# Max and exp of a softmax straight from PSUM, and a new order of work in a slot

## The chip, the cores and the metric

The kernel runs on one core of one Trainium2 chip. The metric is the device time of one execution in microseconds (us).

The engines are written as in the profile: PE is TensorE (matmuls; its weight loads are the row PEld), DVE is VectorE, ACT is ScalarE, POOL is GpSimd, SP is SyncE. Each works through its own list of instructions in the order in which the kernel wrote them, and they meet only at semaphores. The kernel gives matmuls eight banks of PSUM.

## The reference, cut to what matters

64 sequences of 128 tokens with 160 channels, each with a context of 77 rows of 256 channels, go through two layers. All is fp32.

```
# first layer ("l0"): 20 heads of 64, twice (self-attention, then attention to the context), then GEGLU
sim  = q @ k.T * 64**-0.5              # self: 128 columns a head; context: 77
attn = softmax(sim);  x = x + (attn @ v) @ wo + bo
x    = (h * gelu(gate)) @ w2 + b2 + x

# second layer ("l1"): 20 heads of 8; 73 text rows and 4 image rows of the context
p_t  = softmax(q @ k_t.T * 8**-0.5)    # 73 columns a head
qsem = l2norm(p_t @ text);  sem = qsem @ l2norm(image).T
p_ip = softmax(q @ k_ip.T * 8**-0.5 + 0.5 * sem) * mask
out  = (p_t @ v_t + p_ip @ v_ip) @ W_out + b_out + x
```

## The kernel before

**Groups, slots and units.** The 64 sequences are worked through in 16 groups of four. A *unit* is the softmax of four heads: a unit of the first layer is two heads of two sequences (40 a group: 20 of the self-attention, 20 of the context), a unit of the second layer is four heads of one sequence (20 a group). Time is cut into *slots*, `STEP = 60` a group, one unit in each. `UNIT_AT` says which: the second-layer units of a group stand in slots 4, 5, 7, 8, 10, 11, 13, 14, 16, 17, 22, 24, 27, 30, 33, 37, 42, 47, 50 and 53 of the group *after* it, and first-layer units in the other 40. For the last group the 20 second-layer units stand alone (slots 4 to 13 and 20 to 29), with no first-layer work around them.

**The pipeline of a unit.** Every engine runs one loop over the slots `t`, and in each slot it does a different stage of several units. Before, for the unit of slot u: PE computes its scores into one of two banks `PS` in slot u-1; DVE takes the maximum, subtracts it into the buffer `SE` (four buffers) and, for a second-layer unit, copies the image scores away (`softmax_in`, slot u); ACT takes the exponential of `SE` in place (`exp`, slot u); for first-layer units DVE sums and inverts (`prob_sums`) and POOL multiplies (`normalise`), slot u+1; PE transposes the probabilities into the bank `PT` (`probs_transposed`, slot u+2), ACT copies them to `PTs` (`pt_out`); PE multiplies them by the values into the bank `PV` (`probs_v`, slot u+3); for a first-layer unit ACT copies `PV` out (`ot_out`, slot u+4) and PE applies `wo`; for a second-layer unit DVE reads `PV` (`unit_out`, slot u+4: a reciprocal, three small products, one product over 292 columns that ends in `on_done`, one sum of squares).

**Product bank.** `PVS` has one bank. So `probs_v` of a unit waits until the unit before it has been read: by ACT (`ots_done`) or, where that was a second-layer unit, by DVE (`on_done`, the fifth instruction of `unit_out`, L940).

**Jobs.** Everything else that PE computes goes through three general banks `PG` in the order of `JOBS`: the projections of q and k for the first-layer unit two slots ahead (`qk`), and the "late" jobs at a slot's end: values (`v`, one for two units), transposes of the normalised input (`xT`), feed-forward (`ff`, `down`, in slots 55 to 58 and 68 to 71 of a group), and the second layer's own. In slots 55 to 57 and 68 to 70 ACT goes between Gelu and Exp, each with a table load.

**Order before, within slot t.** PE: scores(t+1), transposes(t-2), qk(t+2), wo(t-4), products(t-3), late jobs. ACT: ot_out(t-4), pt_out(t-2), qk copies(t+2), exp(t), tails, late jobs. DVE: unit_out(t-4), softmax_in(t), prob_sums(t-1), block_out(t-4), late jobs, layer norms, tails. POOL: normalise(t-1), layer norms, and once per sequence of the second layer one `pow` over 20 columns.

## Time and profile before

| | |
|---|---|
| median of 3 runs | 4817.66 us (4814.41 to 4827.26) |
| the profiled execution: time, span | 4820.58 us, 4818.8 us |
| busy share of the span: PE, DVE, ACT, POOL | 89%, 63%, 51%, 21% |
| mean granted clock of PE | 0.925 of full speed |
| first scores of the groups 8 and 9 | 2326.6 us and 2620.1 us |

The profiled execution lasted 1.8 us more than its span, and is 3 us above the median. A group takes 293.5 us in the middle of the run (287 us for some). A busy PE is not PE at its peak, since matmuls overlap. The granted clock is 1.0 (2.4 GHz) or 0.5 (1.2 GHz); a value between them is a mixture over the stretch.

### The profile page before, as it was taken

Reading aid. Unit: us, or ns where it says so; the run is one execution under the profiler, and the core shown is the slowest. Engines: PE = TensorE matmul, PEld = TensorE weight load, DVE = VectorE, ACT = ScalarE, POOL = GpSimd, SP = SyncE. Lnnn points to the kernel's source line nnn. Section 1 sums busy time; section 2 is a strip of 40 time slices with the busy share of each in tenths; the row PEclk is TensorE's granted clock in tenths of the full one; section 3 lists DMA queues with packets and bytes.
Section 4 is the critical chain, followed back from the end, with each engine's and each line's share of the span. In section 5 each row is a group of like instructions: output and inputs, shape, how many; then the busy total and the mean of one; then the engine's idle time right before and its main releaser. Section 6 shows DMA issues by size and latency. Waiting matters only on the chain.

```text
span 4818.8 us, 85960 instructions
## 1 busy us (share of the span) xinstructions
PE 4271.6 (89%) x31232; PEld 3694.5 (77%) x31232; DVE 3024.9 (63%) x9036; ACT 2435.6 (51%) x5493; POOL 1013.4 (21%) x1079
## 2 busy tenths in 40 slices
PE   1898988999899998999999899898999999999997
PEld 1787877878787787877878788787877878777776
DVE  3556675666666666665666656666676666656654
ACT  2455554545555554554545545455554545545442
POOL 0222222122222222222122212221122122212211
PEclk9999999999999999989999999999999999899995
DMA  4000000000000000000000000000000000000000
GB/s 113 3 3 7 3 7 3 6 4 3 7 3 6 4 4 6 3 6 3 6 4 3 6 3 6 4 3 6 4 5 4 4 5 3 7 2 5 4 3 3
DMA packets 34030, 34.27 MB, mean 7 GB/s; under 512 B 4336, under 2 KB 31824, under 8 KB 33616
## 3 DMA queue, kind: packets, MB, share of 16 engines
q1 hardware_dynamic: 26752, 25.47, 1.9%
q10 hardware_dynamic: 6864, 3.30, 0.4%
q8 instruction: 257, 4.21, 0.4%
q14 instruction: 157, 1.29, 0.1%
HBM read 23.52 MB, written 5.24 MB: 6 GB/s over the span
## 4 chain that ended last, share of the span: by engine, by line
PE 67%; DVE 18%; issue 7%; ACT 3%; POOL 3%; POOLq 0%; DVEq 0%; DMA 0%; ACTq 0%
PE PT L595 8%; PE PW L558 6%; PE PS L571 6%; PE PG L451 5%; PE PV L609 5%; PE PV L619 5%; PE PG L443 5%; PE PS L580 4%; DVE mx L896 3%; PE PG L426 3%; PE PG L429 3%; PE PG L427 3%; PE PG L428 3%; DVE SE L900 2%; POOL SE L1037 2%
## 5 line engine op out<-in xcount | busy, mean ns | idle before, releaser
L1037 POOL TENSOR_TENSOR SE<-SE,rs 128x512 f32<-128x512 f32 (+1 forms) x640 | 559.0, 873 | 3168.1 <-DVE rs L918 3168.0
L699 ACT ACTIVATE PTs<-PT 77x512 f32<-77x512 f32 (+2 forms) x960 | 571.3, 595 | 1073.8 <-PE PT L595 1073.2
L706 ACT ACTIVATE SE<-SE 128x308 f32<-128x308 f32 (+2 forms) x960 | 491.4, 512 | 488.8 <-DVE SE L900 367.8
L595 PE MATMUL PT<-ident,SE 128*128 128x128 f32 (+2 forms) x3840 | 653.7, 297 | 79.1 <-POOL SE L1037 79.0
L595 PEld LDWEIGHTS PT<-ident,SE 128*128 128x128 f32 (+2 forms) x3840 | 482.7, 153 | 294.9 <-POOL SE L1037 151.7
L827 DVE COPY v_sb<-PG 128x512 f32<-128x512 f32 (+1 forms) x320 | 220.1, 688 | 746.5 <-PE PG L451 416.2
L571 PE MATMUL PS<-qk 128*128 128x154 f32 (+1 forms) x2560 | 583.7, 350 | 59.5 <-ACT qk L660 30.4
L609 PE MATMUL PV<-PTs,v_sb 128*64 128x128 f32 (+1 forms) x5120 | 441.4, 295 | 120.6 <-issue 87.3
L900 DVE TENSOR_TENSOR SE<-PS,mx 128x308 f32<-128x308 f32 (+2 forms) x960 | 522.2, 544 | 33.0
L896 DVE TENSOR_REDUCE mx<-PS 128x4 f32<-128x308 f32 (+2 forms) x960 | 508.8, 530 | 18.1 <-PE PS L571 15.1
L558 PE MATMUL PW<-w_o,OTs 128*128 128x160 f32 x2560 | 500.4, 321 | 10.2 <-ACT OTs L691 10.2
L571 PEld LDWEIGHTS PS<-qk 128*128 128x128 f32 x2560 | 404.7, 192 | 122.1 <-issue 40.7
L609 PEld LDWEIGHTS PV<-PTs,v_sb 128*64 128x64 f32 (+1 forms) x5120 | 284.3, 142 | 231.5 <-issue 181.6
L660 ACT ACTIVATE qk<-PG 64x164 f32<-64x164 f32 (+1 forms) x1280 | 426.9, 334 | 7.5
L658 ACT ACTIVATE qk<-PG 128x256 f32<-128x256 f32 x640 | 246.0, 384 | 351.2 <-PE PG L443 194.1
L558 PEld LDWEIGHTS PW<-w_o,OTs 128*128 128x128 f32 x2560 | 403.7, 206 | 16.1 <-ACT OTs L691 15.2
L619 PE MATMUL PV<-gv,PTs 73*128 73x86 f32 x2560 | 363.3, 289 | 54.1 <-DVE SE L940 48.3
L619 PEld LDWEIGHTS PV<-gv,PTs 73*128 73x128 f32 x2560 | 350.3, 209 | 66.8 <-ACT PTs L699 50.1
L580 PE MATMUL PS<-kbd,q1T 32*128 32x308 f32 x640 | 282.4, 524 | 105.0 <-DVE SE L900 79.2
L913 DVE TENSOR_REDUCE sums<-SE 128x4 f32<-128x512 f32 (+1 forms) x640 | 364.6, 570 | 12.0 <-ACT SE L706 12.0
L443 PE MATMUL PG<-cT,w_kc 128*128 128x164 f32 x1920 | 270.8, 280 | 0.0
L451 PE MATMUL PG<-w_vc,cT 128*77 128x256 f32 x1920 | 261.3, 285 | 0.0
(204 smaller groups left out, 8133.8 us busy)
## 6 DMA issues: line engine op xcount, KB each, us to landing
xres<-in_x_dram SPq DMA_DIRECT2D x32, 160.0 KB, 2.4
out_dram<-x SPq DMA_DIRECT2D x64, 80.0 KB, 1.6
shared<-in_ctx_dram SPq DMA_DIRECT2D x32, 154.0 KB
w_o<-in_L_xattn_a_wo_dram ACTq DMA_DIRECT2D x2, 800.0 KB, 11.5
SE<-in_L_xattn_a_wq_dram SPq DMA_DIRECT2D x2, 640.0 KB, 4.7
qk<-in_L_xattn_a_wq_dram SPq DMA_DIRECT2D x8, 160.0 KB, 4.7
SE<-in_L_xattn_a_wk_dram SPq DMA_DIRECT2D x2, 640.0 KB, 4.0
SE<-in_L_xattn_a_wv_dram SPq DMA_DIRECT2D x2, 640.0 KB, 3.8
```

Of the source, the lines that this page charges most:

```text
L443: last = mm(ps, w[:, c, hw, c0:c0 + 128], cT[:, c, hc, HB * TS * h:HB * TS * (h + 1)], start=(c == 0 and i == 0), stop=(c == 1 and i == 2))
L451: last = mm(ps, cT[:, c, hc, TS * b:TS * b + rows], w[:, c, hw, c0:c0 + n], start=(c == 0 and i == 0), stop=(c == 1 and i == 2))
L558: last = mm(PW[:, C * b:C * b + C], OTs[:, n % 2, 128 * b:128 * b + 128], w_o[n // U0][:, p, :], start=(p == 0 and b == 0), stop=(p == NP ...
L571: last = mm(ps[:, 2 * J * b:2 * J * b + 2 * J], qk[:, n % 2, 0, 128 * b:128 * b + 128], qk[:, n % 2, 1:3, kstep * b:kstep * b + J], start= ...
L595: last = tr(PT[0:J, 128 * i:128 * i + 128], SE[:, place % 4, J * i:J * i + J], ident[:, :])
L609: last = mm(PV[DH * e:DH * e + DH, 128 * b:128 * b + 128], v_sb[0:J, n // 2 % 2, b, 2 * (n % 2) + e, :], PTs[0:J, place % 2, 128 * i:128 * ...
L619: last = mm(PV[:, GV * i + off:GV * i + off + GS + D1], PTs[0:TT, place % 2, 128 * i:128 * i + 128], gv[:, b % 2, 2 * w + i // 2, off:off ...
L699: a_(PTs[0:J, place % 2, :], PT[0:J, :], ACT.Copy).then_inc(S["pts_done"], 1)
L706: a_(e, e, ACT.Exp, scale=scale).then_inc(S["exp_done"], 1)
L896: v.tensor_reduce(mx[:, place % 2, :], sc[:, :, 0:J], AX, ALU.max).then_inc(S["mx_done"], 1)
L900: last = v.tensor_tensor(e.rearrange("p (i j) -> p i j", j=J), sc[:, :, 0:J], mx[:, place % 2, :].unsqueeze(2).to_broadcast([128, 4, J]), ...
L1037: gp.tensor_tensor(e, e, rs[:, n % 2, :].unsqueeze(2).to_broadcast([128, 4, J]), ALU.mult)\
```

## The change

No count of banks changes: three `PG` and one `PV` stand in both kernels. What changes:

- **Softmax.** DVE writes the maximum negated and no longer subtracts. ACT computes exp(score + bias) straight from the bank `PS` with four instructions, one a head, whose bias is a column of `mx`. The scale moves into the copies of q (`SCALE0`, `SCALE1`). `sub_done` is gone: the bank `PS` is released by `exp_done`, and for second-layer units also by `sip_in`, the copy of the image scores.
- **Lags.** Transposes come one slot after a unit's slot instead of two, products two instead of three, outputs three instead of four (`PT_LAG`, `PV_LAG`, `OUT_LAG`); sums and normalisation move from slot t+1 to slot t, the maximum from t to t-1, `v` jobs from t+1 to t, and the tails of a sequence follow its last unit one slot sooner.
- **Order.** PE: scores(t+1), qk(t+2), transposes(t-1), wo(t-3), products(t-2), late. ACT: ot_out(t-3), exp(t), qk copies(t+2), pt_out(t-1), tails, late. DVE: prob_sums(t), softmax_in(t+1), unit_out(t-3), block_out(t-3), the rest as before. POOL: normalise(t), layer norms, and norms_of(t-3).
- **Norms.** The `pow` over 20 columns per sequence becomes one over 4 columns after each second-layer unit (`norms_of`, into the new buffer `n20`).

```diff
+    PT_LAG, PV_LAG, OUT_LAG = 1, 2, 3
...
-            return STEP * (g + 1) + l1_slots(g)[W1 * b + W1 - 1] + 6
+            return STEP * (g + 1) + l1_slots(g)[W1 * b + W1 - 1] + OUT_LAG + 2
...
-            [(t + 1, ("v", u[1], u[2] // 2)) for t, u in UNIT_AT.items() if u[0] == "l0" and u[2] % 2 == 0]
+            [(t, ("v", u[1], u[2] // 2)) for t, u in UNIT_AT.items() if u[0] == "l0" and u[2] % 2 == 0]
...
                 def scores(u):
                     place, (layer, g, n) = PLACE[u], u
                     if place >= 2:
-                        pe.wait_ge(S["sub_done"], place - 1)
+                        pe.wait_ge(S["exp_done"], place - 1)
+                        layer0, g0, n0 = UNITS[place - 2]
+                        if layer0 == "l1":
+                            pe.wait_ge(S["sip_in"], l1_count(g0, n0))
...
                     if t + 1 in UNIT_AT:
                         scores(UNIT_AT[t + 1])
-                    if t - 2 in UNIT_AT:
-                        probs_transposed(UNIT_AT[t - 2])
                     for name in qk_at(t):
                         job(name)
-                    if l0_at(t - 4) is not None:
-                        wo(*l0_at(t - 4)[1:])
-                    if t - 3 in UNIT_AT:
-                        probs_v(UNIT_AT[t - 3])
+                    if t - PT_LAG in UNIT_AT:
+                        probs_transposed(UNIT_AT[t - PT_LAG])
+                    if l0_at(t - OUT_LAG) is not None:
+                        wo(*l0_at(t - OUT_LAG)[1:])
+                    if t - PV_LAG in UNIT_AT:
+                        probs_v(UNIT_AT[t - PV_LAG])
...
-                        a_(qk[:, i % 2, 0, :], ps[:, 0:HT], ACT.Copy)
+                        a_(qk[:, i % 2, 0, :], ps[:, 0:HT], ACT.Copy, scale=SCALE0)
...
                 def exp(u):
                     place, (layer, g, n) = PLACE[u], u
-                    act.wait_ge(S["sub_done"], place + 1)
-                    J, scale = (K0[n // U0], SCALE0) if layer == "l0" else (TT, SCALE1)
-                    e = SE[:, place % 4, 0:4 * J]
-                    a_(e, e, ACT.Exp, scale=scale).then_inc(S["exp_done"], 1)
+                    act.wait_ge(S["mx_done"], place + 1)
+                    if place >= 4:
+                        act.wait_ge(S["pt_done"], place - 3)
+                        layer0, g0, n0 = UNITS[place - 4]
+                        if layer0 == "l1":
+                            act.wait_ge(S["qq_done"], l1_count(g0, n0))
+                    J, step = (K0[n // U0],) * 2 if layer == "l0" else (TT, T)
+                    if layer == "l1":
+                        act.wait_ge(S["sip_in"], l1_count(g, n))
+                    for i in range(4):
+                        last = a_(SE[:, place % 4, J * i:J * i + J], PS[place % 2][:, step * i:step * i + J], ACT.Exp,
+                                  bias=mx[:, place % 2, i:i + 1])
+                    last.then_inc(S["exp_done"], 1)
...
-                    if l0_at(t - 4) is not None:
-                        ot_out(UNIT_AT[t - 4])
-                    if t - 2 in UNIT_AT:
-                        pt_out(UNIT_AT[t - 2])
+                    if l0_at(t - OUT_LAG) is not None:
+                        ot_out(UNIT_AT[t - OUT_LAG])
+                    if t in UNIT_AT:
+                        exp(UNIT_AT[t])
                     for name in qk_at(t):
                         job(name)
-                    if t in UNIT_AT:
-                        exp(UNIT_AT[t])
+                    if t - PT_LAG in UNIT_AT:
+                        pt_out(UNIT_AT[t - PT_LAG])
...
-                    v.tensor_reduce(mx[:, place % 2, :], sc[:, :, 0:J], AX, ALU.max).then_inc(S["mx_done"], 1)
-                    dve.wait_ge(S["mx_done"], place + 1)
-                    if place >= 4:
-                        dve.wait_ge(S["pt_done"], place - 3)
-                    last = v.tensor_tensor(e.rearrange("p (i j) -> p i j", j=J), sc[:, :, 0:J],
-                                           mx[:, place % 2, :].unsqueeze(2).to_broadcast([128, 4, J]), ALU.subtract)
+                    v.tensor_reduce(mx[:, place % 2, :], sc[:, :, 0:J], AX, ALU.max, negate=True).then_inc(S["mx_done"], 1)
...
-                    if t - 4 in UNIT_AT and l0_at(t - 4) is None:
-                        unit_out(UNIT_AT[t - 4])
-                    if t in UNIT_AT:
-                        softmax_in(UNIT_AT[t])
-                    if l0_at(t - 1) is not None:
-                        prob_sums(UNIT_AT[t - 1])
+                    if l0_at(t) is not None:
+                        prob_sums(UNIT_AT[t])
+                    if t + 1 in UNIT_AT:
+                        softmax_in(UNIT_AT[t + 1])
+                    if t - OUT_LAG in UNIT_AT and l0_at(t - OUT_LAG) is None:
+                        unit_out(UNIT_AT[t - OUT_LAG])
...
+                def norms_of(g, k):
+                    b, w = k // W1, k % W1
+                    pool.wait_ge(S["qq_done"], l1_count(g, k))
+                    if w == 0 and GB * g + b >= 2:
+                        pool.wait_ge(S["tail_part"], 4 * (GB * g + b - 2) + 1)
+                    gp.tensor_tensor(n20[:, b % 2, 4 * w:4 * w + 4], qq[:, b % 2, 4 * w:4 * w + 4], p_half[:, 0:4], ALU.pow)\
+                        .then_inc(S["n20_done"], 1)
...
-                    if l0_at(t - 1) is not None:
-                        normalise(UNIT_AT[t - 1])
+                    if l0_at(t) is not None:
+                        normalise(UNIT_AT[t])
...
-                    for g, b, part in tails_at(t):
-                        if part == -1:
-                            pool.wait_ge(S["qq_done"], W1 * (GB * g + b + 1))
-                            gp.tensor_tensor(r20[:, 0, :], qq[:, b % 2, :], p_half[:, :], ALU.pow).then_inc(S["n20_done"], 1)
+                    if t - OUT_LAG in UNIT_AT and l0_at(t - OUT_LAG) is None:
+                        norms_of(*UNIT_AT[t - OUT_LAG][1:])
```

## Rows read from the trace of the kernel before

**Rows 1.** The page, part 1: busy us (share of the span) and instructions.
```profile
PE 4271.6 (89%) x31232; PEld 3694.5 (77%) x31232; DVE 3024.9 (63%) x9036; ACT 2435.6 (51%) x5493; POOL 1013.4 (21%) x1079
```

**Rows 2.** The view of the cores: span, and mean granted TensorE clock.
```profile
core 0: 4818.8 us, clock 0.925
```

**Rows 3.** The waits of PE: total us, times, longest us.
```profile
PE PV L609 <- issue: 87.3, 60, 2.2
PE PS L580 <- DVE SE L900: 79.2, 105, 1.8
PE PT L595 <- POOL SE L1037: 79.0, 123, 2.7
PE PV L619 <- DVE SE L940: 48.3, 48, 2.7
...
PE PS L571 <- ACT qk L660: 30.4, 52, 1.2
...
PE PS L571 <- DVE SE L900: 17.9, 19, 1.0
```

**Rows 4.** Groups of DVE by form: busy us, mean ns of one, idle before.
```profile
L900 DVE TENSOR_TENSOR SE<-PS,mx 128x512 f32<-128x512 f32 x320 | 221.3, 692 | 11.1
L896 DVE TENSOR_REDUCE mx<-PS 128x4 f32<-128x512 f32 x320 | 216.7, 677 | 15.8 <-PE PS L571 14.8
...
L896 DVE TENSOR_REDUCE mx<-PS 128x4 f32<-128x308 f32 x320 | 148.8, 465 | 1.4 <-PE PS L571 0.3
...
L918 DVE RECIPROCAL rs<-sums 128x4 f32<-128x4 f32 x640 | 114.0, 178 | 22.0
```

**Rows 5.** Groups of ACT by form, same columns.
```profile
L706 ACT ACTIVATE SE<-SE 128x512 f32<-128x512 f32 x320 | 201.7, 630 | 282.8 <-DVE SE L900 279.3
...
L706 ACT ACTIVATE SE<-SE 128x308 f32<-128x308 f32 x320 | 146.9, 459 | 93.0 <-DVE SE L900 88.5
...
L706 ACT ACT_TABLE_LOAD x96 | 123.2, 1283 | 1.7
...
L668 ACT ACTIVATE shared<-PG,b 128x256 f32<-128x256 f32 x160 | 72.8, 474 | 38.4 <-PE PG L429 37.1
```

**Rows 6.** Groups of POOL by form, same columns.
```profile
L1057 POOL TENSOR_TENSOR r<-qq,p_half 128x20 f32<-128x20 f32 x64 | 226.6, 3540 | 97.1 <-DVE qq L942 97.1
...
L1019 POOL TENSOR_TENSOR rstd<-vp,p_mhalf 128x2 f32<-128x2 f32 x96 | 68.7, 716 | 8.0
```

**Rows 7.** Timeline of PE, slots 40 and 42 of group 8: start us, us, what.
```profile
2528.07 0.69 PE L571 MATMUL PS<-qk 128*128 128x154 f32 x4
...
2528.59 0.60 PE L595 MATMUL PT<-ident,SE 128*77 128x128 f32 x4
...
2529.03 0.71 PE L558 MATMUL PW<-w_o,OTs 128*128 128x160 f32 x4
...
2536.93 0.37 PE L426 MATMUL PG<-nT,w_q_hi 128*128 128x256 f32 x1
...
2538.14 0.74 PE L558 MATMUL PW<-w_o,OTs 128*128 128x160 f32 x4
```

**Rows 8.** Timeline of PE, a slot that begins with first-attention scores.
```profile
2393.77 1.03 PE L571 MATMUL PS<-qk 128*128 128x256 f32 x4
2394.63 0.60 PE L595 MATMUL PT<-ident,SE 128*128 128x128 f32 x4
```

**Rows 9.** Timeline, a wait for the product bank.
```profile
2469.41 0.18 DVE L928 RECIPROCAL rr<-PV 128x4 f32<-128x4 f32 x1
...
2469.88 0.45 DVE L940 TENSOR_TENSOR SE<-PV,SE 128x292 f32<-128x292 f32 x1
...
2470.43 0.66 PE L609 MATMUL PV<-PTs,v_sb 128*64 128x128 f32 x8 [2.24 <-issue]
```

**Rows 10.** Windows after that wait, and around one of 1.78 us: busy, PEclk, DMA.
```profile
2475.00:2480.00 5.00, 5.00 (x35) 4.34 (x34) 0.30 (x3) 2.52 (x6) 1.04 (x1) 0.62 0.00 0
2590.00:2595.00 5.00, 3.22 (x31) 2.92 (x31) 3.68 (x13) 2.20 (x6) 0.24 (x1) 1.00 0.00 0
```

More of the change, by code:

```diff
@@ L131, in xattn_program @@
         r20 = sb("r20", [128, 4, H])
+        n20 = sb("n20", [128, 2, H])
         o1 = sb("o1", [128, 2, H, D1])
@@ L268, in xattn_program @@
                  "qk_done", "v_done",
-                 "s_done", "mx_done", "sub_done", "exp_done", "sum_done", "p_done", "pt_done", "pts_done", "pv_done", "rs_done", "rr_done",
+                 "s_done", "mx_done", "sip_in", "exp_done", "sum_done", "p_done", "pt_done", "pts_done", "pv_done", "rs_done", "rr_done",
                  "on_done", "ots_done", "wo_done", "x_done",
@@ L670, in job @@
                     elif kind == "q1":
-                        a_(q1T[:, i, :, :].rearrange("p r n -> p (r n)"), take(name)[:, :], ACT.Copy)\
+                        a_(q1T[:, i, :, :].rearrange("p r n -> p (r n)"), take(name)[:, :], ACT.Copy, scale=SCALE1)\
                             .then_inc(S["q1_done"], 1)
@@ L905, in softmax_in @@
                             dve.wait_ge(S["job_full"], JOB[("ipT",) + divmod(GB * g + b - 2, GB)] + 1)
-                        last = v.tensor_copy(sip[:, b % 2, 4 * w:4 * w + 4, :], sc[:, :, TT:T])
-                    last.then_inc(S["sub_done"], 1)
+                        v.tensor_copy(sip[:, b % 2, 4 * w:4 * w + 4, :], sc[:, :, TT:T]).then_inc(S["sip_in"], 1)
                 def prob_sums(u):
@@ L947, in image_scores @@
                     if part == 0:
-                        dve.wait_ge(S["n20_done"], j + 1)
-                        then(v.tensor_tensor(r20[:, 1, :], r20[:, 0, :], rr[:, k, :], ALU.mult))
+                        dve.wait_ge(S["n20_done"], W1 * (j + 1))
+                        then(v.tensor_tensor(r20[:, 1, :], n20[:, k, :], rr[:, k, :], ALU.mult))
                         then(v.tensor_scalar(r20[:, 2, :], r20[:, 1, :], EPS_L2, None, ALU.max))
@@ L955, in image_scores @@
                                                     r20[:, 3, :].unsqueeze(2).to_broadcast([128, H, NIP]), ALU.mult, ALU.mult))
-                        v.scalar_tensor_tensor(e, e, SCALE1, sem4[:, k, :, :], ALU.mult, ALU.add)\
+                        v.tensor_tensor(e, e, sem4[:, k, :, :], ALU.add)\
                             .then_inc(S["tail_part"], 1)
@@ L978, in _ @@
                 for t in range(FIRST, LAST):
-                    if t - 4 in UNIT_AT and l0_at(t - 4) is None:
-                        unit_out(UNIT_AT[t - 4])
-                    if t in UNIT_AT:
-                        softmax_in(UNIT_AT[t])
-                    if l0_at(t - 1) is not None:
-                        prob_sums(UNIT_AT[t - 1])
-                    if l0_at(t - 4) is not None and l0_at(t - 4)[2] % NP == NP - 1:
-                        block_out(*l0_at(t - 4)[1:])
+                    if l0_at(t) is not None:
[4 more added lines that the diff above has]
+                        unit_out(UNIT_AT[t - OUT_LAG])
+                    if l0_at(t - OUT_LAG) is not None and l0_at(t - OUT_LAG)[2] % NP == NP - 1:
+                        block_out(*l0_at(t - OUT_LAG)[1:])
                     for g, h in preps_at(t):
```

1 line of the change is left out of this document (removed).

## Prediction

> **What bounds the kernel now.** I read the page's busy times first, then the view of the cores, the waits of PE, the timeline of two groups, and the windows around its stalls. The reader is to see in turn: who is the bound, how fast it is clocked, whom it waits for, what stands ahead of that in the other engine's queue, and what a stall does to the clock.
>
> PE is busy 4271.6 of 4818.8 us and no other engine comes near [rows 1]. So the end is set by PE's list of work, PE's stalls, and PE's clock. The mean granted clock is 0.925 [rows 2]; with levels 1.0 and 0.5 that is (1 - 0.925) / 0.5 = 15% of the span at the lower one, some 720 us, and about half of it, 360 us, is what the clock costs. The change alters no matmul. It can win or lose only in the stalls and, through them, the clock.
>
> The stalls fall into two families [rows 3]:
> - *Softmax not ready.* Scores wait for the subtraction that frees their bank: 79.2 + 17.9 = 97.1 us. Transposes wait for POOL's product: 79.0 us. Scores wait for the copies of q and k: 30.4 us. Together 206.5 us.
> - *Product bank not free.* The second-layer products wait 48.3 us for DVE's L940, the read that ends in `on_done`. The 87.3 us called "issue" ahead of L609 are the same wait as I read them: in the timeline L940 ends at 2470.33 and the products start at 2470.43, after 2.24 us [rows 9]. Together 135.6 us, or 8.5 us a group.
>
> **The work added and removed.** DVE loses the subtraction: 960 instructions, of 692 ns in the 512-wide form [rows 4] and less in the others; with about 0.55 us for the mean that is some 520 us, and DVE falls from 63% to about 52%. It isn't the bound, so this is worth nothing by itself; what counts is where DVE is late.
>
> ACT replaces one exponential of 630 or 459 ns [rows 5] by four. The trace has none of these, so I bound them. From the two widths the cost is (630 - 459) / (512 - 308) = 0.84 ns a column; the Gelu, which like the new exponential reads PSUM and takes a bias per partition, costs 474 ns at 256 columns, hence about 366 ns at 128 and 324 ns at 77. Four end to end are at most 1.46 and 1.30 us; at least they cost what the one instruction costs now, 0.63 and 0.46. Back-to-back instructions overlap a little, so I take 1.3 and 1.15 us, near the upper end. Added: 960 times 0.65 to 0.7 us, some 640 us; ACT rises from 51% to about 64%. It lies beside PE's work, unless ACT's order makes the copies of q and k late (a rival below). Table loads (1283 ns) stay as many, since only the first of the four needs one.
>
> POOL: `pow` takes 716 ns over 2 columns and 3540 over 20 [rows 6], so about 1.03 us over 4; 320 of these instead of 64 long ones are 330 us against 227. POOL is at 21%, and the long one, which stood in the way of the next normalisation, is gone. The lags, the `v` job a slot sooner and the folded scales cost nothing in work: the same instructions are issued, and no DMA moves apart from the stores, one slot sooner after each sequence.
>
> **What goes away.** Scores(t+1) now wait for exp(t-1), which comes a whole slot before. The transposes get the sums of their own slot and stand behind qk, so they come about 1.2 us later in PE's slot. I take away 90% of 97.1 + 79.0, and half of the 30.4: 158 + 15 = -173 us.
>
> **What grows: the wait for the one product bank.** In slot t PE's products(t-2) need `on_done` of the unit of slot t-3 when that is a second-layer unit: 20 times a group. Before, the matching `unit_out` was DVE's *first* item in the slot. Now it stands behind prob_sums(t), which waits for exp(t), and behind the maximum of the unit t+1, whose scores PE only begins in this slot. PE's own position in the slot is unchanged. Worked out from the slot's start T:
>
> - Slot 40 (first-layer context unit; unit 37 is second-layer; no qk, no wo). PE: scores 0.52 us, transposes 0.44 [rows 7], so it wants the product bank at T + 0.96. DVE: ACT finishes the preceding `pt_out` at about T + 0.15, exp(40) at T + 1.3; sums 0.47 (width as the maximum's 465 ns) and reciprocal 0.18 make about 2.0; maximum 0.47 [rows 4] makes 2.5; `unit_out` up to `on_done` takes 2470.33 - 2469.41 = 0.92, with semaphores 1.05 [rows 9], so 3.5. PE waits 2.5 us.
> - Slots where t is itself a second-layer unit have no sums. With self-attention scores next (0.86 us [rows 8], results some 0.2 later), maximum 0.68 and `unit_out` 1.05 give T + 2.9. Without a qk job PE is there at 1.3 and waits 1.6 us (slots 8, 11, 14: 4.8 us). With one (1.21 us, [rows 7], self-attention's about 1.0) it waits 0.4 to 0.6 or not at all (slots 7, 10, 13, 16, 17, 27, 30, 33, 50, 53: 3.8 us).
> - The seven slots of the first kind by the same sum: 19: 1.8; 20: 2.1; 25: 2.7; 36: 1.0; 40: 2.5; 45: 2.4; 56: 3.0 (here exp stands behind Gelus and a table load of 1.28 [rows 5]). Sum 15.5 us. What differs among them: 19, 20 and 25 are 512 wide (exp 1.3, sums and reciprocal 0.86, maximum 0.68); in 19, 36 and 56 a qk job keeps PE busy for 1.0 to 1.2 us of it; in 20 and 36 exp is done before T, and DVE is held by the copy of the values instead, until about T + 0.9.
>
> Total 24 us a group at full clock; at the lower clock, 15% of the time, PE arrives later, so I take 22. Against 8.5 now: +13.5 x 16 = +216 us.
>
> **The clock.** After the 2.24 us stall above the window 2475 to 2480 shows a granted clock of 0.62; around the stall of 1.78 us it stays 1.00 [rows 10]. So a longer stall is dearer than its own length. The new sum has nine stalls of 1.6 us and more a group. Now 720 / 16 = 45 us a group are spent at the lower clock; I put 6 to 7 us more: half of it, times 16, is +50 us.
>
> The Trainium skill, "TensorE: Matmul & The Clock Gate", section "HAM oscillation — how this bites in real kernels", says that regular idle gaps return the clock to half rate again and again. By it each of the nine stalls would bring one drop, which is the third rival below.
>
> **The end.** The last group's 20 second-layer units stand alone; the wait grows there too, by about 1 us in some 15 slots, against the last `pow` (2.5 us less) and a slot less of lag: +10 us.
>
> **Sum.** 4820.6 (the profiled execution's time, 3 us above the median) - 173 + 216 + 50 + 10 = 4923 us, and 4920 against the median: slower by 2.1%. Its own range is 4835 to 5000.
>
> **Rivals.**
> - *Faster: `unit_out` isn't late enough to matter.* DVE has 0.55 us a slot less to do and ACT may be done with exp(t) well before T. If the wait grows by 4 us a group instead of 13.5, that is +64; with -173 and a fifth of the clock's 360 us given back (-72), and nothing at the end, 4640 us. It decides from a growth below 11 us a group (173 / 16), and more surely below 8. For it: the backlog of DVE causes the present stalls, and each slot of backlog now holds one subtraction less. Against: the sum for slot 40 holds even with DVE idle before it. Range 4560 to 4805. Chance 0.31.
> - *Same: both families cancel.* PE's list stays at 4271.6 us and the stalls only move. 4818, chance 0.10. The Trainium skill, "Perfetto Trace Analysis", section "Identifying Performance Opportunities", holds that improvement comes from the most-contended engine; by that rule, with PE's work untouched, moving work from DVE to ACT gives this time.
> - *Much slower: the clock.* If each of the nine long stalls brings 7 us at the lower level (63 a group instead of 45, of which half, 9 us, is time and 3 of it are in the forecast) and the stalls are a third larger (+7 a group), that is 4923 + 16 x (6 + 7) = 5130 us. Chance 0.10.
> - *Much slower: ACT.* qk copies now stand behind exp(t). If they end 0.3 us after PE wants to begin the next scores in most of the 640 first-layer slots, +190 us on the forecast: 5110. Against it: exp(t) should end at T + 1.7 with ot_out ahead, before the qk job is through at about T + 2. Chance 0.06.
>
> **How the numbers follow.** The forecast has 0.43. About 0.3% is what a measurement of this kernel can tell from no change. Slower: 0.43 + 0.10 + 0.06 = 0.59; same 0.10; faster 0.31. The range 4640 to 5060 leaves out some 0.1 at either end.
>
> **What would show it.** Right: "issue" or L940 ahead of PE's product matmuls (L609, L619 of before) at some 300 to 380 us in PE's waits instead of 135.6; a wait of over 2 us in slots 25, 40 and 45 of each group; DVE's order there sums, maximum, reciprocal; waits of scores and of transposes below 50 us in all; the four exponentials together 1.1 to 1.3 us; ACT at 64%. Wrong: if DVE's `on_done` in slot 40 comes less than 2 us after the slot's scores begin, the forecast's main term falls; if the mean clock rises above 0.94, the clock's sign is wrong; if ACT's copies of q and k head the waits, it is the last rival.

## The result and the profile after

The changed kernel takes 4655.07 us (median of 4 runs, 4645.55 to 4656.96) against 4816.03 us: ratio 0.9662, 95% interval 0.9635 to 0.9689. It is 3.4% faster. I had forecast 2.1% slower; the time lies at the lower end of the range.

The profiled execution took 4653.59 us. The page's part 1 (it answers to [rows 1]) and the view of the cores ([rows 2]):

```profile
PE 4146.7 (89%) x31232; PEld 3600.3 (77%) x31232; DVE 2535.2 (54%) x8076; ACT 2832.9 (61%) x8373; POOL 1106.4 (24%) x1335
```

```profile
core 0: 4651.9 us, clock 0.949
```

The span fell by 4818.8 - 4651.9 = 166.9 us. It splits in two, because both kernels run the same 31232 matmuls. PE's idle time (span less busy) went from 547.2 to 505.2 us: -42. PE's busy time went from 4271.6 to 4146.7 us: -125, and that is the clock. A stretch at half clock costs half its length, so the clock costs (1 - mean) x span: 0.075 x 4818.8 = 361 us before, 0.051 x 4651.9 = 237 us after, -124.

PE's waits, in the columns of [rows 3]. L615 and L625 are the products of first- and second-layer units, L601 the transposes, L577 the first layer's scores:

```profile
PE PV L615 <- ACT PTs L705: 155.4, 103, 2.7
...
PE PV L615 <- issue: 91.5, 106, 3.0
PE PV L625 <- DVE SE L948: 85.7, 73, 3.1
PE PV L625 <- issue: 13.1, 17, 1.2
...
PE PT L601 <- POOL SE L1053: 7.8, 10, 1.3
PE PS L577 <- ACT qk L666: 5.2, 9, 1.1
```

The softmax family of the prediction has all but gone: 206.5 us became 7.8 + 5.2 = 13. The rows ahead of products sum to 345.7 us (347 with a row of 1.5). Three releasers are named, but in the trace every one of these 301 gaps ends 0.1 to 0.2 us after L948, the `on_done` of the changed kernel: all of them are the wait for the product bank. Slot 40 of group 8, the slot that the prediction worked out, in the timeline (start us, us, engine, line, what):

```profile
2443.36 0.95 ACT L719 ACTIVATE SE<-PS,mx 128x77 f32<-128x77 f32 x4
...
2443.60 0.72 PE L577 MATMUL PS<-qk 128*128 128x154 f32 x4
...
2444.16 0.60 PE L601 MATMUL PT<-ident,SE 128*77 128x128 f32 x4
2444.34 0.47 DVE L921 TENSOR_REDUCE sums<-SE 128x4 f32<-128x308 f32 x1 [1.02 <-ACT SE L719]
...
2444.85 0.18 DVE L926 RECIPROCAL rs<-sums 128x4 f32<-128x4 f32 x1
2444.95 0.45 DVE L910 TENSOR_REDUCE mx<-PS 128x4 f32<-128x308 f32 x1
...
2445.31 0.17 DVE L936 RECIPROCAL rr<-PV 128x4 f32<-128x4 f32 x1
...
2445.77 0.45 DVE L948 TENSOR_TENSOR SE<-PV,SE 128x292 f32<-128x292 f32 x1
...
2446.32 0.66 PE L615 MATMUL PV<-PTs,v_sb 77*64 77x128 f32 x8 [1.56 <-ACT PTs L705]
```

T is 2443.60, where PE starts the scores of the slot. The four exponentials end at T + 0.71, the sums run at T + 0.74, the reciprocal, the maximum at T + 1.35, `unit_out` from T + 1.71, L948 ends at T + 2.62, and PE's products start at T + 2.72 after 1.56 us. The order is the one forecast and PE's own arrival too (2446.32 - 1.56 = T + 1.16, by 0.96); ACT was 0.6 us sooner than I had put it, so the stall is 1.6 us and not 2.5.

The new instructions, ACT and POOL by form (columns of [rows 5]). I had put four exponentials at 1.3 us (128 columns) and 1.15 us (77); from the first's start to the fourth's end they took 1.14 and 0.97 us (medians of 320; 0.95 in slot 40). So ACT's busy time rose by 397 us (2435.6 to 2832.9) where I had put 640. The `pow` had been put at 1.03 us:

```profile
L719 ACT ACTIVATE SE<-PS,mx 128x128 f32<-128x128 f32 x1280 | 363.6, 373 | 22.3 <-DVE qq L950 14.6 <-DVE mx L910 7.5
L719 ACT ACTIVATE SE<-PS,mx 128x77 f32<-128x77 f32 x1280 | 309.7, 332 | 11.1 <-DVE mx L910 10.4
```

```profile
L1045 POOL TENSOR_TENSOR n<-qq,p_half 128x4 f32<-128x4 f32 x320 | 323.4, 1011 | 836.2 <-DVE qq L950 836.2
```

And the clock, in windows (us, busy of PE, PEld, DVE, ACT, POOL, then the granted clock, DMA). Before, around a wait of 1.43 us ahead of second-layer scores, whose timeline row comes first:

```profile
2345.49 1.14 PE L580 MATMUL PS<-kbd,q1T 32*128 32x308 f32 x2 [1.43 <-issue]
```

```profile
2340.00:2345.00 5.00, 4.06 (x33) 3.36 (x31) 4.29 (x10) 2.35 (x6) 0.29 (x2) 1.00 0.00 0
2345.00:2350.00 5.00, 4.51 (x19) 3.08 (x20) 4.24 (x13) 1.99 (x5) 1.91 (x2) 0.57 0.00 0
2350.00:2355.00 5.00, 5.00 (x19) 3.95 (x20) 3.09 (x11) 0.82 (x2) 1.87 (x4) 0.50 0.02 5
```

After, around one of its long waits:

```profile
2386.57 0.66 PE L615 MATMUL PV<-PTs,v_sb 128*64 128x128 f32 x8 [2.62 <-issue]
```

```profile
2385.00:2390.00 5.00, 3.43 (x28) 2.87 (x28) 3.56 (x14) 2.28 (x8) 2.35 (x3) 1.00 0.00 0
2390.00:2395.00 5.00, 4.58 (x41) 4.27 (x39) 2.98 (x12) 2.81 (x10) 0.73 (x1) 1.00 0.00 0
```

A wait of 1.43 us in the kernel before is followed by some 10 us at or near half clock, through a window in which PE is busy for all its 5 us. One of 2.62 us in the changed kernel leaves the clock at 1.00. So a single stall's length doesn't fix its price. But the second case is an exception, as all stretches at half clock show when they are counted in the two traces, from the first scores to those of the last group (103.5 to 4371.2 us before, 103.2 to 4213.9 after). Each is set against the last wait of PE, of over 0.15 us, that began before it; every stretch begins during that wait or at most 2.1 us after its end.

| | before | after |
|---|---|---|
| stretches at half clock | 83, 546 us in all | 67, 314 us in all |
| mean length of a stretch | 6.6 us | 4.7 us |
| its last wait is ahead of scores or transposes | 77 | 0 |
| its last wait is ahead of products | 6 | 67 |
| two or more waits in the 5 us before it | 59 | 0 |
| waits over 2 us that are such a last wait | 6 of 16 | 38 of 42 |
| waits of 1.6 to 2 us, the same | 2 of 31 | 23 of 33 |
| waits of 1 to 1.6 us | 37 of 75 | 6 of 67 |
| waits of 0.5 to 1 us | 38 of 224 | 0 of 67 |

In the changed kernel long waits, each alone, bring the falls of the clock. In the kernel before most falls come behind short waits that stand close together, and the last of them is nearly always one for the softmax; in 30 of the 83 the longest of the waits in the 5 us before is one ahead of products. The last group, where the mean clock is 0.81 in both, adds much the same to each (175 and 166 us at half clock). So the clock's gain lies in the middle of the run.

### The profile page after: what moved, and what is told of

It reads as the page before. It is cut to its first block, busy times and chain, and to the rows that moved or that the text cites. A ratio compares the mean times of both kernels' runs of the same rounds, so it can differ in the third digit from the quotient of the medians.

```text
span 4651.9 us, 88382 instructions
## 1 busy us (share of the span) xinstructions
PE 4146.7 (89%) x31232; PEld 3600.3 (77%) x31232; DVE 2535.2 (54%) x8076; ACT 2832.9 (61%) x8373; POOL 1106.4 (24%) x1335
## 3 DMA queue, kind: packets, MB, share of 16 engines
q14 instruction: 174, 1.43, 0.1%
## 4 chain that ended last, share of the span: by engine, by line
PE 77%; DVE 8%; issue 6%; ACT 6%; POOL 2%; ACTq 0%; DMA 0%; DVEq 0%; POOLq 0%
PE PS L577 10%; PE PV L615 8%; PE PT L601 8%; PE PW L561 7%; PE PG L454 6%; PE PV L625 6%; PE PG L446 5%; PE PG L429 4%; PE PS L586 4%; PE PG L432 3%; PE PG L430 3%; PE PG L431 3%; ACT SE L719 2%; PE PG L509 2%; PE PG L478 2%
## 5 line engine op out<-in xcount | busy, mean ns | idle before, releaser
L719 ACT ACTIVATE SE<-PS,mx 128x128 f32<-128x128 f32 (+2 forms) x3840 | 978.1, 343 | 81.5 <-DVE sip L915 45.3
L615 PE MATMUL PV<-PTs,v_sb 128*64 128x128 f32 (+1 forms) x5120 | 429.7, 288 | 246.9 <-ACT PTs L705 155.4
L601 PE MATMUL PT<-ident,SE 128*128 128x128 f32 (+2 forms) x3840 | 616.6, 286 | 7.9 <-POOL SE L1053 7.8
L577 PE MATMUL PS<-qk 128*128 128x154 f32 (+1 forms) x2560 | 603.9, 359 | 5.6 <-ACT qk L666 5.2
L615 PEld LDWEIGHTS PV<-PTs,v_sb 128*64 128x64 f32 (+1 forms) x5120 | 278.0, 138 | 368.6 <-issue 184.8
L601 PEld LDWEIGHTS PT<-ident,SE 128*128 128x128 f32 (+2 forms) x3840 | 471.6, 151 | 72.8 <-issue 43.7
L1045 POOL TENSOR_TENSOR n<-qq,p_half 128x4 f32<-128x4 f32 x320 | 323.4, 1011 | 836.2 <-DVE qq L950 836.2
L842 DVE COPY v_sb<-PG 128x512 f32<-128x512 f32 (+1 forms) x320 | 219.9, 687 | 493.9 <-PE PG L454 308.2
L561 PE MATMUL PW<-w_o,OTs 128*128 128x160 f32 x2560 | 472.9, 309 | 9.7 <-ACT OTs L697 9.6
L577 PEld LDWEIGHTS PS<-qk 128*128 128x128 f32 x2560 | 415.0, 196 | 65.6 <-issue 43.8
L625 PE MATMUL PV<-gv,PTs 73*128 73x86 f32 x2560 | 355.6, 285 | 100.3 <-DVE SE L948 85.7
L625 PEld LDWEIGHTS PV<-gv,PTs 73*128 73x128 f32 x2560 | 339.1, 203 | 121.1 <-issue 85.6
L561 PEld LDWEIGHTS PW<-w_o,OTs 128*128 128x128 f32 x2560 | 383.7, 198 | 16.3 <-ACT OTs L697 16.1
L697 ACT ACTIVATE OTs<-PV 128x256 f32<-128x256 f32 x640 | 242.4, 379 | 134.7 <-PE PV L615 127.3
L454 PE MATMUL PG<-w_vc,cT 128*77 128x256 f32 x1920 | 280.6, 298 | 0.0
L586 PE MATMUL PS<-kbd,q1T 32*128 32x308 f32 x640 | 266.8, 498 | 11.7 <-issue 11.7
## 6 DMA issues: line engine op xcount, KB each, us to landing
w_o<-in_L_xattn_a_wo_dram ACTq DMA_DIRECT2D x2, 800.0 KB, 11.7
```

The source lines that it names most:

```text
L454: last = mm(ps, cT[:, c, hc, TS * b:TS * b + rows], w[:, c, hw, c0:c0 + n], start=(c == 0 and i == 0), stop=(c == 1 and i == 2))
L561: last = mm(PW[:, C * b:C * b + C], OTs[:, n % 2, 128 * b:128 * b + 128], w_o[n // U0][:, p, :], start=(p == 0 and b == 0), stop=(p == NP ...
L577: last = mm(ps[:, 2 * J * b:2 * J * b + 2 * J], qk[:, n % 2, 0, 128 * b:128 * b + 128], qk[:, n % 2, 1:3, kstep * b:kstep * b + J], start= ...
L586: last = mm(ps[:, 0:4 * T], q1T[row:row + 32, h, r, 128 * (b % HB):128 * (b % HB) + 128], kbd[row:row + 32, r, b % HB, :, :].rearrange("p ...
L601: last = tr(PT[0:J, 128 * i:128 * i + 128], SE[:, place % 4, J * i:J * i + J], ident[:, :])
L615: last = mm(PV[DH * e:DH * e + DH, 128 * b:128 * b + 128], v_sb[0:J, n // 2 % 2, b, 2 * (n % 2) + e, :], PTs[0:J, place % 2, 128 * i:128 * ...
```

## The experiments

Times are medians; each ratio is to the kernel before, run on the same chip. Line numbers differ a little from one version to the next.

**out_first: `unit_out` back in front.** All else as changed.

```diff
+                    if t - OUT_LAG in UNIT_AT and l0_at(t - OUT_LAG) is None:
+                        unit_out(UNIT_AT[t - OUT_LAG])
                     if l0_at(t) is not None:
                         prob_sums(UNIT_AT[t])
                     if t + 1 in UNIT_AT:
                         softmax_in(UNIT_AT[t + 1])
-                    if t - OUT_LAG in UNIT_AT and l0_at(t - OUT_LAG) is None:
-                        unit_out(UNIT_AT[t - OUT_LAG])
```

> The changed kernel with unit_out moved back to the first place of DVE's slot; all else as changed. Theory 1 (the product bank is held too long because unit_out stands third): nearly all stalls of PE in the changed kernel stand ahead of products (347 us of PE's waits); with unit_out first they fall to 100 to 170 us, while waits for scores and transposes rise from 13 to at most 60 us. PE's idle time falls by 130 to 200 us, and if each us less of stall gives back half a us by the clock, the kernel takes 4350 to 4480 us. Rival (the order is neutral: what unit_out gains, the sums and the normalisation lose, and transposes wait instead): 4640 to 4670 us, with over 150 us of waits ahead of transposes.

Measured: 4325.02 us, ratio 0.8971 (0.8952 to 0.8990). The page's part 1 and the waits:

```profile
PE 4024.6 (93%) x31232; PEld 3493.4 (81%) x31232; DVE 2540.2 (59%) x8076; ACT 2822.8 (65%) x8373; POOL 1100.0 (25%) x1335
```

```profile
PE PV L625 <- DVE SE L948: 46.2, 40, 2.7
PE PV L615 <- ACT PTs L705: 38.7, 31, 1.6
PE PV L615 <- issue: 34.8, 68, 1.1
PE PT L601 <- POOL SE L1053: 12.7, 25, 1.3
...
PE PV L625 <- issue: 6.1, 16, 0.7
```

Waits ahead of products fell from 347 to 125.8 us, and transposes rose only from 7.8 to 12.7. PE's idle time fell by 505.2 - 291.8 = 213 us, the clock (0.978) gave 237 - 95 = 142 us. The waits are in the expected range; the idle time fell by more than the 130 to 200 us expected and the time is below the 4350 to 4480, since the clock gave back about two thirds of a us for each us of idle time and not half. The changed kernel's third place for `unit_out` costs 4655 - 4325 = 330 us, 7.6% on top of the better order. This version beats both kernels.

**out_second: sums, `unit_out`, maximum.**

```diff
                         prob_sums(UNIT_AT[t])
+                    if t - OUT_LAG in UNIT_AT and l0_at(t - OUT_LAG) is None:
+                        unit_out(UNIT_AT[t - OUT_LAG])
                     if t + 1 in UNIT_AT:
                         softmax_in(UNIT_AT[t + 1])
-                    if t - OUT_LAG in UNIT_AT and l0_at(t - OUT_LAG) is None:
-                        unit_out(UNIT_AT[t - OUT_LAG])
```

> The changed kernel with DVE's order sums(t), unit_out(t-3), maximum(t+1): of the two things that stand ahead of unit_out, the maximum goes behind it. The working of the prediction gives the stalls: where t is a second-layer unit (8.6 us a group) nothing is ahead any more, and in the seven slots where t is a first-layer unit 15.5 us shrink by a maximum, 0.5 to 0.7 each, to 11. So waits ahead of products fall from 347 us to 180 to 230 us, and the kernel takes 4420 to 4520 us. Rival (the maximum itself, and not the sums that wait for the exponential, is what holds unit_out): waits under 150 us, as with unit_out first, and 4325 to 4380 us.

Measured: 4450.42 us, ratio 0.9232 (0.9218 to 0.9246).

```profile
PE PV L615 <- ACT PTs L705: 107.2, 74, 2.4
...
PE PV L625 <- DVE SE L948: 59.7, 40, 2.8
PE PV L615 <- issue: 53.2, 59, 2.4
...
PE PV L625 <- issue: 6.1, 16, 0.7
```

226.2 us ahead of products, within the 180 to 230 worked out, and the time within its range too. The two things ahead of `unit_out` each hold it: the maximum accounts for 347 - 226 = 121 us of waits, the sums behind the exponential for 226 - 126 = 100.

**two_banks: the other way to free the products.** Two product banks, two general ones.

```diff
-        PG = [... for i in range(3)]
+        PG = [... for i in range(2)]
...
-        PVS = [... for i in range(1)]
+        PVS = [... for i in range(2)]
```

> The changed kernel with two product banks and two general banks. Theory 1 (one product bank is what all stalls of the changed kernel wait for): waits ahead of products fall from 347 us to under 80; new waits ahead of the general jobs, since the copies out of a general bank must now keep up with every second job. If those stay under 150 us the kernel takes 4450 to 4600 us. Rival (general banks are as scarce as the product bank): waits ahead of jobs of over 300 us, 4660 us or more.

Measured: 4326.65 us, ratio 0.8970 (0.8955 to 0.8986), below the 4450 to 4600 that I expected. No wait ahead of products is left in the list. PE's waits ahead of general jobs are new (L842 copies the values out, L429 begins a qk or ff job):

```profile
PE PG L429 <- DVE v_sb L842: 52.2, 30, 2.2
PE PG L429 <- DVE x L860: 21.1, 15, 1.4
PE PG L509 <- DVE v_sb L842: 16.6, 16, 1.1
```

With four smaller rows (12.9, 5.5, 5.3 and 3.8) they are 117 us, of which 4 were there in the changed kernel. Two edits with nothing in common but the product bank take away its waits and come to 4325 and 4327 us; that they agree to 2 us is chance, since each leaves other waits. That the wait for the product bank is what costs the changed kernel 330 us is shown.

**softmax_only: the subtraction gone, old lags and order.** Edits of `softmax_in`, `exp`, `scores` and the folded scales, as in the change.

```diff
+                    for i in range(4):
+                        last = a_(SE[:, place % 4, J * i:J * i + J], PS[place % 2][:, step * i:step * i + J], ACT.Exp,
+                                  bias=mx[:, place % 2, i:i + 1])
```

> The kernel before with only the softmax changed: maximum negated, four exponentials straight from PSUM, scales folded into q; lags and order as before. Theory S (DVE without the subtraction is what made the change faster): softmax waits fall from 206 us to under 80 and the backlog behind the product bank shrinks too, 4600 to 4700 us. Theory O (lags and order made it faster, and here the longer exponential stands behind the qk copies in ACT's slot, so scores wait for it through the bank PS): 4800 us or more.

Measured: 4949.67 us, ratio 1.0268 (1.0246 to 1.0289), slower than before. Scores now wait for the exponential, which frees their bank (L574, L583: scores; L716: exponential):

```profile
PE PS L574 <- ACT SE L716: 190.7, 223, 2.3
PE PS L583 <- ACT SE L716: 178.1, 199, 2.6
```

368.8 us, against 97.1 for the subtraction in [rows 3]. In the old order the exponential stands behind the copies of q and k in ACT's slot. This is Theory O's case.

**sub_dve: the subtraction back on DVE, new lags and order.** From out_first.

```diff
-                    for i in range(4):
-                        last = a_(SE[:, place % 4, J * i:J * i + J], PS[place % 2][:, step * i:step * i + J], ACT.Exp,
-                                  bias=mx[:, place % 2, i:i + 1])
+                    a_(e, e, ACT.Exp).then_inc(S["exp_done"], 1)
...
+                    last = v.tensor_tensor(e.rearrange("p (i j) -> p i j", j=J), sc[:, :, 0:J],
+                                           mx[:, place % 2, :].unsqueeze(2).to_broadcast([128, 4, J]), ALU.subtract)
```

> The kernel out_first with the subtraction back on DVE and one exponential in place; lags, order and norms as changed, unit_out first. Theory S: 0.55 us of DVE a slot costs most of the gain back, 4700 us or more, with waits ahead of products over 200 us. Theory O: the order and the lags carry the gain, and it stays within 60 us of out_first.

Measured: 4340.26 us, ratio 0.8998 (0.8982 to 0.9014):

```profile
PE 4014.7 (93%) x31232; PEld 3490.2 (81%) x31232; DVE 3023.5 (70%) x9036; ACT 2373.6 (55%) x5493; POOL 1101.9 (25%) x1335
```

DVE carries 3023.5 us here and 2540.2 in out_first; the times are 15 us or 0.4% apart and the intervals of their ratios overlap. The lags and an order with `unit_out` first, together with the scales folded into q and the `pow` a unit, which sub_dve keeps, make the kernel before 10% faster with the subtraction still on DVE. The move of the subtraction, the part that names the change, is worth next to nothing there, and costs 2.7% in the old order. What it is worth in the changed kernel's own order, where the subtraction would stand ahead of `unit_out`, no run shows.

**max_early and exp_second: which part of the order.** Two steps from softmax_only: first the maximum a slot sooner, then the exponential ahead of `pt_out` and the copies of q and k.

```diff
-                    if t in UNIT_AT:
-                        softmax_in(UNIT_AT[t])
+                    if t + 1 in UNIT_AT:
+                        softmax_in(UNIT_AT[t + 1])
...
+                    if t in UNIT_AT:
+                        exp(UNIT_AT[t])
                     if t - 2 in UNIT_AT:
                         pt_out(UNIT_AT[t - 2])
                     for name in qk_at(t):
                         job(name)
-                    if t in UNIT_AT:
-                        exp(UNIT_AT[t])
```

> The kernel softmax_only (exponential straight from PSUM, old order) with one thing of the new order: DVE takes the maximum of the unit t+1 in slot t instead of that of unit t. Theory O1 (what the lags and the order bring is that the softmax starts a slot sooner, so the bank PS comes free before PE needs it): the waits of scores for the exponential fall from 369 us to under 80, and the kernel takes 4450 to 4650 us. Rival O2 (it is ACT's order, the exponential behind the copies of q and k, that holds the scores): waits stay over 200 us and the time over 4800 us.

Measured: 4822.41 us, ratio 1.0017 (1.0007 to 1.0027). Waits of scores for the exponential:

```profile
PE PS L574 <- ACT SE L716: 176.1, 221, 2.3
...
PE PS L583 <- ACT SE L716: 90.6, 138, 1.1
```

> The kernel max_early with ACT's order as in the change as well: ot_out(t-4), exp(t), pt_out(t-2), copies of q and k. Lags of transposes, products and outputs as before. Theory O2 (the scores wait for the exponential because it stands behind the copies of q and k): waits of scores for ACT's exponential fall from 267 us to under 60. If the two steps together are what the new order brings, 4400 to 4550 us; if the shorter lags and qk ahead of the transposes carry a part of their own, or the copies of q and k now come late, 4600 us or more, with waits of scores for L663 or of transposes above 80 us.

Measured: 4773.62 us, ratio 0.9896 (0.9875 to 0.9918). The last letters of each row say who released PE (L663: copies of k):

```profile
PE PS L574 <- ACT qk L663: 135.0, 120, 2.2
...
PE PS L583 <- ACT SE L716: 62.5, 79, 1.1
PE PT L598 <- POOL SE L1042: 61.4, 83, 2.3
```

The maximum's slot took the 369 us to 267, so Theory O1 fell and its rival O2 held. The exponential's place took them to 62.5, as O2 has it, but then PE waited 135 us for the copies of q and k ahead of scores (with 26 more ahead of jobs), and transposes waited 61: the second of the two cases expected, over 4600 us. In the full order PE issues qk ahead of the transposes, so ACT has its input sooner and the transposes come later in the slot; out_first has all of that, and 4325 us. How much of the rest comes from PE's order, how much from the shorter lags (the sums a slot sooner among them) and how much from the small `pow` was not separated.

The two also say something of the clock. PE stands idle for longer in them than in the kernel before (592 and 567 us, span less busy, against 547), and yet the clock is 0.940 and 0.941 against 0.925.

**keep_busy: the waits filled with work.** From the changed kernel. The repeated transposes compute nothing new.

```diff
+    AGAIN = {7: 3, 8: 2, 11: 2, 14: 2, 19: 3, 20: 2, 25: 4, 40: 3, 45: 2, 50: 3, 56: 4}
...
-                        probs_transposed(UNIT_AT[t - PT_LAG])
+                        probs_transposed(UNIT_AT[t - PT_LAG], AGAIN.get(t % STEP, 0))
...
-                    for i in range(4):
+                    for i in [0] * (4 * again) + list(range(4)):
                         last = tr(PT[0:J, 128 * i:128 * i + 128], SE[:, place % 4, J * i:J * i + J], ident[:, :])
```

> The changed kernel, but in eleven slots of a group in which PE waits 0.8 to 2.7 us for the product bank (7, 8, 11, 14, 19, 20, 25, 40, 45, 50, 56) PE repeats the four transposes of that slot two to four times into the same bank, 0.8 to 1.7 us of work in place of waiting. The extra work computes nothing new. Theory C (the clock falls because PE stood still just before): PE's busy time in wall terms rises but the waits fall by as much, the mean granted clock rises from 0.949 to over 0.965, and the kernel gets 40 to 120 us faster: 4535 to 4615. Rival (the clock doesn't answer to the stalls, or the repeated transposes hold up ACT's copy and so the next exponential): clock within 0.005 of 0.949 or time at 4655 or above.

Measured: 4534.6 us, ratio 0.9427 (0.9409 to 0.9445). The view of the cores and PE's waits:

```profile
core 0: 4536.6 us, clock 0.986
```

```profile
PE PV L616 <- issue: 57.0, 149, 0.8
PE PV L616 <- ACT PTs L706: 54.7, 59, 1.2
PE PV L626 <- DVE SE L949: 48.9, 73, 2.4
PE PV L626 <- issue: 12.8, 17, 0.8
```

The kernel does 1932 matmul instructions more and is 120 us faster, at the edge of the 4535 to 4615 expected. Waits ahead of products fell to 173.4 us and the clock rose from 0.949 to 0.986; it costs 0.014 x 4536.6 = 64 us instead of 237, and of the 67 stretches at half clock in the middle of the run one is left. The 173 us gained there less 4655 - 4535 = 120 leave some 53 us that the added work cost beyond the waits that it filled. That the changed kernel loses clock to its stalls is shown: filling them in eleven slots gave back 173 of the 237 us.

**shift2, shift4, after_shift2, after_shift4: is the clock luck?** The transposes of slot 48, where PE doesn't wait, are repeated twice or four times, in the kernel before and in the changed one. They compute nothing new, and only move what comes later.

```diff
-                        probs_transposed(UNIT_AT[t - 2])
+                        probs_transposed(UNIT_AT[t - 2], 2 if t % STEP == 48 else 0)
...
-                    for i in range(4):
+                    for i in [0] * (4 * again) + list(range(4)):
```

> The kernel before, with the four transposes of slot 48 of each group repeated twice, 0.9 us of PE work where PE doesn't wait: 16 times, 14 us in all. The extra work computes nothing new. Theory A (what the clock costs follows from how the stalls are spread within a group): the time moves by 0 to +14 us, the mean clock stays within 0.005 of 0.925. Theory B (it is a matter of where the stalls happen to fall in time, so any shift redraws it): the clock moves by over 0.008 and the time by over 30 us to either side.

> As shift2, but repeated four times, 1.8 us a group, 28 us in all. Theory A: 0 to +28 us, clock within 0.005 of 0.925. Theory B: clock off by over 0.008, time off by over 30 us beyond the 28, and not in line with shift2.

> The changed kernel with the four transposes of slot 48 of each group repeated twice, as in shift2: 0.9 us of PE work a group where PE doesn't wait, 14 us in all; nothing new is computed. If the changed kernel's better clock (0.949 against 0.925 at nearly the same idle time) belongs to how its stalls lie, the clock stays within 0.005 of 0.949 and the time is 4655 to 4670 us. If it was luck with where the stalls fell in time, the clock moves towards 0.93 to 0.94 and the time to over 4690 us.

> As after_shift2 with four repeats, 28 us in all. Belonging to how the stalls lie: clock within 0.005 of 0.949, 4655 to 4685 us. Luck: clock off by over 0.008, and a time over 30 us outside that.

Measured: shift2 4829.87 us, ratio 1.0038 (1.0015 to 1.0062); shift4 4787.45, 0.9964 (0.9938 to 0.9990); after_shift2 4666.83, 0.9678 (0.9663 to 0.9692); after_shift4 4689.49, 0.9731 (0.9714 to 0.9747). Span and clock of the four, in this order:

```profile
core 0: 4827.2 us, clock 0.926
```

```profile
core 0: 4792.8 us, clock 0.936
```

```profile
core 0: 4654.5 us, clock 0.953
```

```profile
core 0: 4682.4 us, clock 0.947
```

shift2 came out as Theory A has it, and both shifts of the changed kernel kept their clock (after_shift4 is 4 us over its range). shift4 came out as Theory B: by the estimate above it does 28 us more work, and it is 29 us faster, since its clock is 0.936; the waits of the kernel before are still there in it (71.9 us ahead of L580, 78.5 ahead of L595). So the clock's cost at nearly the same stalls moves by some 50 us with where they fall. It moves from one execution to the next as well: the ten of shift2 have 0.917 to 0.931 and 4803 to 4858 us, the ten of shift4 0.928 to 0.940 and 4776 to 4824 us. But no execution of the kernel before or of its two shifts was above 0.940, and none of the changed kernel or its two was below 0.946. The profiled ones have 0.925, 0.926 and 0.936 against 0.949, 0.953 and 0.947, means 0.021 apart, about 100 us. Most of the 124 us belongs to the change, not to luck.

## Why the prediction was wrong

- **What bounds the kernel: right.** PE's stalls and its clock moved, its work didn't.
- **Where the stalls would be: right, though not slot by slot.** Of 23.7 us of idle time a group (mean of groups 2 to 14, gaps between matmuls), 22.2 us fall in the twenty slots named; the sum taken was 22. By class, forecast against measured:

```
slots                                  forecast us   measured us
t second-layer, no qk: 8, 11, 14             4.8           3.4
t second-layer, others (ten slots)           3.8           7.4
t first-layer (seven slots)                 15.5          11.5
all twenty                             24, taken 22       22.2
```

  That the total is so close is in part luck, since the classes miss to both sides. The ten others are mostly slots 7 and 50, with 2.5 and 1.7 us, which my sum put at 0.6 or less each; I take it that Gelu or norm work is in the way there, but that wasn't followed up. Of the seven, 25 and 56 came out at 2.65 and 2.7 us, while 40 and 45 had 1.6 and 1.3 us where the sum had 2.5 and 2.4. The sign "over 2 us in slots 25, 40 and 45" held in one of the three.
- **What goes away: 173 forecast, 193.5 measured** (206.5 to 13.0), a term sized low by 20 us.
- **The growth at the product bank: +216 forecast, +175 measured.** The end value was right (352 forecast, 347 measured); the start value was low. I counted 135.6 us and left out the rows of products released by "ACT PTs", 30.7 and 5.8 us; in the trace of the kernel before these gaps too end 0.1 to 0.2 us behind L940. So 172 became 347. The end was put at +10 us; the last group, from its first scores on, took 447.6 us before and 438.0 after, -10. With smaller waits (the "issue" ahead of the second layer's scores fell from 21.4 us to 11.7) the idle time fell by 42 us, where the sum with its term for the end gave +53.
- **The step that failed: the clock, +50 forecast, -124 measured.** "A longer stall is dearer than its own length" was drawn from two stalls [rows 10]. It added a price for the new long stalls and put at nothing the clock that the old softmax stalls cost, though the sum itself takes 173 us of them away. The new long stalls did bring falls, 38 of 42 of those over 2 us. But in the kernel before 77 of the 83 falls in the middle came behind a wait for scores or transposes, and in the changed kernel none does; 83 stretches of 6.6 us became 67 of 4.7. (The 45 us a group at the lower level, taken for the kernel before, was also too much for the middle, where it is 546 / 15 = 36 us, since the last group alone has 175.) Over the whole run the time at the lower level is 0.102 of 4651.9 us against 0.15 of 4818.8. The prediction's own sign for this (a mean clock above 0.94) came true. The clock's term alone is 174 of the 270 us between the sum's 4923 and the profiled 4652, and it alone turns the sign: 4923 - 174 = 4749. The other 95 us are idle time (+53 forecast, -42 measured): 20 in what goes away, 41 in the growth, 20 in the end, the rest in rows left out of the sum. With these alone put right the sum would be 4828, a little slower still. With the clock's cost unchanged it would have been 4873 by my terms and 4777 by the measured idle time.
- **The Trainium skill's rule** ("TensorE: Matmul & The Clock Gate", section "HAM oscillation — how this bites in real kernels") agrees with keep_busy, where the stalls were filled and the clock rose to 0.986. That each of the nine stalls would bring one drop was my reading of it. The trace has that for most waits over 2 us (38 of 42) and for 23 of 33 between 1.6 and 2, but for hardly any shorter one. There were 67 drops in the middle of the run, 4 to 5 a group and not nine, of 4.7 us each and not 7, so the third rival fails.
- **The rival that named the sign** (`unit_out` not late enough) has the measured time in its range, 15 us from its 4640, but its main step was wrong: the wait grew by 175 us and not 64. It was right that exp(t) would be done sooner (T + 0.71 in slot 40) and that the clock would give something back, though for another reason. The rival in which ACT makes the copies late fails: scores wait 5.2 us for them.
- **The rival of no change** fails, since PE's stalls and clock did move. The Trainium skill's rule named with it ("Perfetto Trace Analysis", section "Identifying Performance Opportunities") isn't refuted by that. The most-contended engine here is PE, and with `unit_out` first moving work between DVE and ACT did next to nothing: sub_dve and out_first differ by 483 us of DVE work and 0.4% of time. What the prediction made of it left out that the order of work changes PE's own stalls.

Why the changed kernel's clock is better at nearly the same idle time is settled only in part. The count in the traces fits this: the stalls of the changed kernel come from one cause and stand alone, and those under 1.6 us hardly ever bring a fall, while those of the kernel before come from four (products, scores, transposes, copies) and often two or more within a few us, as the 2.24 us ahead of products and then 0.88 us ahead of scores at 2470 to 2472, and there short ones bring it as well. But no run changed the spacing of the stalls alone, and why a stretch at half clock lasts 6.6 us on average there and 4.7 here stays open.

## What to carry to other kernels

When a pipeline's stages move, write down for each buffer with a single copy who frees it and what stands ahead of that instruction in its engine's queue, in us from the slot's start; here that sum named the slots and came near the total, with errors of about 1 us in single slots, and the cure (put the freeing item first) was worth more than twice the whole change. Keep PE's idle time and its clock apart, as span less busy and (1 - clock) x span. When you put a price on the clock, go through all falls of the clock in the trace and note the wait ahead of each: then a stall that goes away takes its falls with it in the sum, as a new one brings its own. The load of an engine that isn't the bound says little: half a microsecond of work a slot moved off DVE made 0.4% with `unit_out` first, and made the old order slower.

## What the runs showed of the hardware

- In these two kernels each of the 150 stretches at half clock in the middle of the run began during a wait of PE or at most 2.1 us after it, but half clock then lasted through time without any gap, as at 2350 to 2355.
- Filling eleven waits a group with useless transposes raised the granted clock from 0.949 to 0.986 and made the kernel 120 us faster, with 6% more matmul instructions.
- Delaying a group by 1.8 us of work in a slot without a wait moved the mean clock from 0.925 to 0.936 and the time from 4817 to 4787 us. Ten executions of one such kernel ranged over 0.014 of clock and 55 us.
- Four ACT exponentials of 77 columns from PSUM with a bias per partition, 332 ns each, took 0.97 us in a row, not 1.33; four of 128 columns, 373 ns each, took 1.14 us, not 1.49. Neighbours overlap by some 0.12 us.
